# Two attention blocks: where the value matmuls and the row-maximum matmuls of a key tile stand between its scores

## The reference

```python
scores = jnp.einsum('bhqd,bhkd->bhqk', q, k) / jnp.sqrt(jnp.float32(HEAD_DIM))
attn = jax.nn.softmax(jnp.where(causal[None, None], scores, -jnp.inf), axis=-1)   # layer 0, causal
out = jnp.einsum('bhqk,bhkd->bhqd', attn, v)
...
weights = jax.nn.softmax(scores, axis=-1)                                         # layer 1, no mask
out = jnp.einsum('bhqk,bhkd->bhqd', weights, V)
```

## Time and profile before

| | |
|---|---|
| median of 3 runs | 5524.33 us (5508.73 to 5526.52) |
| the profiled execution | 5519.82 us, of which its span is 5518.0 us |
| TensorE matmul busy | 5035.9 us, 91% of the span |
| VectorE busy | 4698.1 us, 85% |
| ScalarE busy | 3736.7 us, 68% |
| mean granted TensorE clock | 0.940 of full speed |

### The profile page before, as it was taken

The page is one execution under the profiler, slowest core; times in us unless marked ns, Lnnn a source line. Parts: engine busy times, 40 slices in busy tenths (PEclk is TensorE's granted clock), DMA queues, the critical chain, the costliest instruction groups (busy, mean ns, idle before and its releaser), DMA issues. The chain is left out here.

```text
span 5518.0 us, 124529 instructions
## 1 busy us (share of the span) xinstructions
PE 5035.9 (91%) x43370; PEld 2086.1 (38%) x43370; DVE 4698.1 (85%) x5343; ACT 3736.7 (68%) x7102; POOL 213.0 (4%) x262
## 2 busy tenths in 40 slices
PE   7589999999999578875999999999999999999777
PEld 4233434433434245542333333333333333333333
DVE  3588879789889689847999999999999999999835
ACT  2068778687787311131888888888888888888523
POOL 3100000000000000030000000000000000000200
PEclk7589999999999789995999999999999999999988
DMA  4301010010010000051100001000100001000000
GB/s 126 102 17 32 11 28 21 14 39 11 11 41 10 24 14 11 5 192 39 39 7 8 5 5 42 8 5 5 27 23 5 5 8 42 5 8 5 4 9 27
DMA packets 152676, 143.01 MB, mean 26 GB/s; under 512 B 72234, under 2 KB 106986, under 8 KB 152042
## 3 DMA queue, kind: packets, MB, share of 16 engines
q1 hardware_dynamic: 152074, 134.93, 8.7%
HBM read 86.84 MB, written 46.66 MB: 24 GB/s over the span
## 5 line engine op out<-in xcount | busy, mean ns | idle before, releaser
L926 DVE TENSOR_REDUCE att_mx<-ps 128x2 f32<-128x1024 f32 (+2 forms) x3335 | 3897.2, 1192 | 288.1 <-PE ps L801 211.1
L907 ACT ACTIVATE att_probs<-ps 128x512 f32<-128x512 f32 (+3 forms) x6400 | 3390.3, 583 | 643.2 <-PE ps L843 198.3
L870 PE MATMUL ps<-att_probs,att_V 128*17 128x256 f32 (+1 forms) x25088 | 1950.7, 385 | 0.0
L843 PE MATMUL ps<-att_Q,K 50*128 50x512 f32 (+3 forms) x6400 | 1676.9, 491 | 42.1 <-ACT att_probs L907 23.3
L801 PE MATMUL ps<-K,att_Q 48*128 48x512 f32 x6670 | 1458.7, 418 | 140.7 <-DMA K<-khi_scratch 82.1
L843 PEld LDWEIGHTS ps<-att_Q,K 50*128 50x128 f32 x6400 | 649.9, 185 | 1384.0 <-ACT att_probs L907 1314.6
L870 PEld LDWEIGHTS ps<-att_probs,att_V 128*17 128x17 f32 x25088 | 424.9, 95 | 1054.9 <-issue 591.7
L801 PEld LDWEIGHTS ps<-K,att_Q 48*128 48x128 f32 x6670 | 667.6, 192 | 230.0 <-DVE att_mx L926 138.0
L887 ACT ACTIVATE att_negT<-ps 32x128 fp32r<-32x128 f32 x66 | 16.6, 251 | 232.3 <-PE ps L811 232.3
L1181 PE MATMUL ps<-wguT,mlp_xqT 128*128 128x512 f32 (+1 forms) x384 | 166.1, 584 | 0.3 <-DVE mlp_h L1284 0.2
L791 PE MATMUL ps<-att_band,att_pick 64*128 64x128 bf16 x2080 | 162.6, 223 | 0.0
(11 more groups left out here) (211 smaller groups left out, 2391.3 us busy)
## 6 DMA issues: line engine op xcount, KB each, us to landing
K<-khi_scratch SPq DMA_DIRECT2D x320, 64.0 KB, 2.3
att_Q<-qhi_scratch SPq DMA_DIRECT2D x272, 64.0 KB, 2.3
att_V<-v_scratch SPq DMA_DIRECT2D x80, 136.0 KB, 2.5
K<-klo_scratch SPq DMA_DIRECT2D x160, 64.0 KB, 2.3
v_scratch<-proj_vpad SPq DMA_DIRECT2D x16, 544.0 KB, 3.4
att_Q<-qlo_scratch SPq DMA_DIRECT2D x136, 64.0 KB, 2.3
att_Q<-att_negT SPq DMA_DIRECT2D x264, 4.0 KB
proj_x<-in_L_attn_x SPq DMA_DIRECT2D x8, 512.0 KB, 5.2
```

Of the source, the lines that this page charges most:

```text
L843: mm = pe.matmul(ring(at)[:, lo:QB], K[rows, u // NQB, j, kt * P:(kt + 1) * P], Q[rows, slot_of(u), j, lo:QB], start=True, stop=not diagonal)
L870: mm = pe.matmul(ps[VW * h:VW * h + HV, 6, lo:(part + 1) * (QB // 2)], V[:, v // NQB, kt, HV * h:HV * (h + 1)], probs[:, (n_key[v] + kt) % ...
L907: act.activation(probs[:, (n_key[u] + kt) % PBUFS, column(h), lo:QB], ring(at)[:, lo:QB], ACT.Exp, scale=SCALE).then_inc(emptied, 1)
L926: dve.tensor_reduce(mx[:, min(u % NQB, 1), :, j, qt, c], ps[:, 2 + 2 * pair:4 + 2 * pair, 0:max_width(u, i) // 2], AX.X, ALU.max).then_inc ...
```

## The change

All maxima of a key tile move behind its fourth score, and both value parts stand behind its second score. A regular tile is then `ss vv ss mm`. The lag tile becomes `ss ss mm vv`. The turned maximum T, which stands five slots behind the last maximum of the next unit, moves with it. No instruction is added or removed.

```diff
-            at.append(min(int(slot) | 1, slots - 1))
+            at.append(min(int(slot) // GH * GH + GH - 1, slots - 1))
...
-                if kt < LAG and h % 2 and u > 0:
-                    out.append(("values", u - 1, keys(u - 1) - LAG + kt, h // 2))
-                elif kt > LAG and h % 2:
-                    out.append(("values", u, kt - LAG, h // 2))
+                if kt < LAG and h == 1 and u > 0:
+                    out += [("values", u - 1, keys(u - 1) - LAG + kt, part) for part in range(2)]
+                elif kt > LAG and h == 1:
+                    out += [("values", u, kt - LAG, part) for part in range(2)]
                 elif kt == LAG and h == GH - 1:
                     out += [("values", u, 0, part) for part in range(2)]
```

## The result

| | before | after |
|---|---|---|
| median | 5521.51 us (4 runs) | 5901.27 us (4 runs, 5888.25 to 5915.27) |
| ratio to before | 1 | 1.0692, 95% interval 1.0661 to 1.0723 |
| span of the profiled execution | 5518.0 us | 5913.3 us |
| first to last score, layer 0 | 1550.5 us | 1689.4 us |
| first to last score, layer 1 | 2562.3 us | 2812.1 us |

The change makes the kernel 6.9% slower. The forecast had the sign and the mechanism, but 5745 us and a range up to 5805: some 155 us are missing in it. Of the 395 us between the two spans, layer 1 holds 250 (forecast 152) and layer 0 139 (forecast 73).

What follows compares the result with a forecast made beforehand. TensorE was taken as the bound, with the three-bank ring's limit hidden by 0.03 us. Layer 1's +152 and layer 0's +73 made 225 us on the profiled 5519.8, so 5745 us, range 5690 to 5805.

Steps and rivals of the forecast that it cites:

- The ring sets the short side: Regular tile: next pair's second score waits for an exponential until 1.19 us; tile 2.60 us, +0.16; chance 0.80.
- The open term, from a late score to the values: Regular tile: distance from the delayed second score to the values, taken as 0.42 us.
- the upper bound: Late score to values: allowance of 0.07 us above 0.42 for an exposed weight load, +88 us on 1252 tiles.
- The drain saved: Values in one run save about 0.12 us a tile; as rival, banks free sooner, 5295 us, chance 0.07.
- It is covered by the ring wait: Second maximum's wait for VectorE puts the next tile's first score at about 0.92 us, still under 1.19.
- +0.26: Lag tile: expected lengthening in us, from having both short distances, 1.19 and then 1.91 where it had 1.64.
- VectorE's gather keeps its lead over T: Turned maximum: VectorE's gather was to stay as far ahead of it as before; no time was added.
- The clock at nothing: Whole kernel: the 225 us sum included no loss from a lower granted TensorE clock.
- that rival: TensorE's 0.37 us wait per tile might bring half speed in stretches: 60 to 110 us more, about 5840; chance 0.06.
- Layer 0: Regular tiles +53, lag tiles +8, masked tiles -13, runs of maxima +25: together +73 us.
- The counts of runs of maxima and of masked tiles: Layer 0: some 16 tiles with four or more maxima, 20 to 25 us; 128 masked tiles gain 0.1 each, 13.
- T and the DMAs: Unit ends in layer 1: later T leaves just enough DMA time, 0 to 0.3 us a unit, taken as 0.

Runs made afterwards that it cites:

- the first experiment: Values in one run behind the second score, maxima left behind the second and fourth scores, against the kernel before: 6026.64 us, ratio 1.0892.
- last of the seam runs: Changed kernel with the gather behind the tile's maxima and the lag tile's values ahead of its maxima: 5788.77 us, 1.0468 to the kernel before.

## Why the prediction was wrong, by its steps

- *The ring sets the short side* (1.19 + 0.42 + 0.99 = 2.60): right, in size too. Shown by the tile of 2.60; by 2.84 with the values alone in one run; by 2.60 kept with most of VectorE's work gone; and, with that work gone too, by 2.38 with exponentials of half the width. The open term, from a late score to the values, was 0.43 (4492.43 to 4492.86): the upper bound wasn't needed.
- *The drain saved:* right in size (0.99 us for sixteen records is 0.11 less than twice 0.55, forecast about 0.12), and worth nothing, since it is saved on the side that then waits. The Trainium skill has a rule for it (TensorEngine Tiling (Array Packing), Key Properties: changing the tiling mode drains the engine). The 0.11 us agrees with it; no row here shows the drain itself. By the rule alone the first experiment should have been faster, and it is 8.9% slower.
- *"It is covered by the ring wait"*, for VectorE's wait: the first step that failed. In a regular tile it is covered: the next first score comes at 0.93 us and the second one has to wait until 1.18 anyway. I used the cover for all tiles. It is absent where something other than a ring-bound score follows the maxima. In the lag tile the values follow (+0.85 for +0.26). In the tile ahead of the turned maximum the gather delays a reduction by 0.9 us, and the second maximum then waits longer than the ring does ("VectorE's gather keeps its lead over T" looked at T only, not at who waits behind the gather). A unit at full clock grew by 5.94 us, forecast 4.75: 1.19 us times 32, about 38 us of the 98 missing in layer 1. About 5 of these are a slip in the sum: 29 x 0.16 is 4.64, not 4.5.
- *The clock at nothing*: the second step that failed, and the larger one. The sum had no term for it, because the lag tiles of the kernel before had the same ring wait at a clock of 1.00; as a rival it had 0.06. It came, but not from the ring waits as that rival had it. In layer 1 it costs 57 - 3 = 54 us, with the 38 above 92 of the 98. Shown: with ring waits in every tile half clock in layer 1 is 10 us (values alone) and 14 us (last of the seam runs); taking VectorE's waits away in layer 1 took it from 160 to 48, moving the gather to 55. Shown too: where it begins. By the profile's times, 26 of its 27 stretches in layer 1 begin in the lag tile (9) or in the next-to-last tile, behind the 0.90 us wait (17); with the gather moved 10 of 11 begin in the lag tile; the one left over is at the pause between the two passes, which the kernel before has too. Not shown: which wait or sum of waits makes it fall. The run with the lag tile apart and the gather moved had 96, more than the gather alone, and smaller maxima left 10 stretches in a lag tile of 3.24 us.
- *Layer 0* (+73): +139. Its miss of 66 us looks like the same two kinds: half clock rose from 65 to 231 us, and at layer 1's price (54 us for 150 more of half clock) that is an estimated 60 us. The gather's move alone brings layer 0 to +89. The counts of runs of maxima and of masked tiles in the forecast were not tested one by one.
- *T and the DMAs* (0 to 0.3 us): right. The wait for the turned maximum's DMAs is 12.1 us in all, 11.8 before.

## What to carry to other kernels

Where a ring of banks is drained by another engine, the time between refills has a floor made of that engine's latency, and unequal stretches of work between refills pay it on the short side while the long side gives nothing back: keep them equal before saving work inside them. A wait that is hidden behind a second wait in the regular stretch must be checked again at each seam, with what stands behind it there. A rare step in the wrong place can cost more than its own length: here one gather between two reductions held up a maximum, and with it moved away half clock in layer 1 fell from 160 to 55 us as well.

## What was not expected of the hardware

A granted clock of 1.2 GHz without long idleness. In the changed kernel such stretches begin in two tiles of a unit, where TensorE's rows show waits of 0.29 us (at 4518.95) and 0.90 us (at 4591.46); a weight load that waits 0.30 us in every tile (0.66 with the values alone in one run) for the length of a layer did not do it. And a reduction's recorded length (1.22 us) isn't its pace: 1.13 us from start to start when its input is ready.
